# Decay differences as bf16 matmuls of cut cumulated decays, and the read decay in the same exponential

## What is computed

```python
def step(h, inp):
    x_t, dt_t, B_t, C_t = inp
    dA = jnp.exp(dt_t * A)
    h = h * dA[:, :, None, None] + jnp.einsum('bh,bhp,bn->bhpn', dt_t, x_t, B_t)
    y = jnp.einsum('bhpn,bn->bhp', h, C_t)
    return (h, y)
# both directions; NHEADS = 2, HEADDIM = 128, D_STATE = 64; dt = softplus(...)
out = (y_fw + y_bw[:, ::-1, :]) @ out_proj_w.T
```

## Time and profile before

| what | value |
|---|---|
| median of 3 runs | 424.61 us (423.61 to 426.65) |
| the profiled execution | 423.88 us |
| its span, first to last instruction | 422.2 us |
| PE busy | 381.2 us (90%) |
| DVE busy | 341.9 us (81%) |
| POOL busy | 321.2 us (76%) |
| ACT busy | 299.6 us (71%) |
| mean granted TensorE clock | 0.988 |

### The profile page before, as it was taken

One profiled execution on the slowest core, in us unless ns is written; L12 is line 12 of the kernel. 1 busy time (PEld: TensorE's weight loads), 2 busy tenths in 40 slices (PEclk: granted clock), 3 DMA queues, 4 the chain that ended last, 5 costly groups with the idle time before them and its releaser, 6 DMA issues. The chain is left out here.

```text
span 422.2 us, 10384 instructions
## 1 busy us (share of the span) xinstructions
PE 381.2 (90%) x3004; PEld 344.8 (82%) x3004; DVE 341.9 (81%) x1031; ACT 299.6 (71%) x866; POOL 321.2 (76%) x486
## 2 busy tenths in 40 slices
PE   8889989997998899699999899889998998999990
PEld 7757878897888798587889788779998887989990
DVE  6687789998879998989779998789688756768880
ACT  3776789797799988678677788898766665444430
POOL 4754894799995989679989889999947777765541
PEclk9999999999999999999999999999999999999996
DMA  8999999999940000001010110003921176888720
GB/s 228 330 334 335 334 336 331 334 334 330 325 127 2 1 2 2 0 2 50 2 53 2 50 51 3 2 0 110 379 68 39 54 216 177 264 253 234 223 78 0
DMA packets 54950, 63.27 MB, mean 150 GB/s; under 512 B 4604, under 2 KB 47996, under 8 KB 54768
## 3 DMA queue, kind: packets, MB, share of 16 engines
q1 hardware_dynamic: 50528, 55.76, 43.9%
q0 software_dynamic: 2784, 6.37, 4.1%
q10 hardware_dynamic: 1584, 0.50, 0.5%
HBM read 20.97 MB, written 42.09 MB: 149 GB/s over the span
## 5 line engine op out<-in xcount | busy, mean ns | idle before, releaser
L721 POOL TENSOR_TENSOR accb<-accb,prod 128x512 f32<-128x512 f32 x48 | 61.3, 1277 | 23.4 <-ACT accb L1144 19.4
L2036 DVE SCALAR_TENSOR_TENSOR bank<-raw,cw,bank 128x512 f32<-128x512 f32 x96 | 72.1, 751 | 2.2 <-ACT bank L1154 0.9
L754 POOL TENSOR_SCALAR lseg<-strict,av 128x128 f32<-128x128 f32 x128 | 47.8, 387 | 6.4 <-DVE av L1995 4.4
L1577 PE MATMUL bank<-skip,cx 128*128 128x128 f32 x256 | 41.2, 284 | 7.7 <-DVE st L2084 7.3
L1813 PE MATMUL bank<-raw 128*128 x312 | 43.5, 283 | 0.9 <-DVE raw L2459 0.9
L1193 ACT ACTIVATE xt<-bank,dtv 128x128 f32<-128x128 f32 x128 | 39.5, 362 | 5.2 <-PE bank L1556 4.9
L1577 PEld LDWEIGHTS bank<-skip,cx 128*128 128x128 f32 x256 | 33.6, 191 | 10.7 <-DVE st L2084 9.8
L955 POOL DMA_INDIRECT routed_rows<-rows,rowat x32 | 33.5, 1045 | 10.8 <-issue 9.1
L1051 POOL DMA_INDIRECT out_dram<-raw x26 | 25.7, 988 | 20.0 <-DVE raw L2485 13.3
L1813 PEld LDWEIGHTS bank<-raw 128*128 128x128 f32 x312 | 38.0, 192 | 1.7 <-issue 1.0
L1593 PE MATMUL bank<-xt,ms 128*128 128x128 f32 x256 | 39.0, 275 | 0.0
(11 more groups left out here) (294 smaller groups left out, 1134.8 us busy)
## 6 DMA issues: line engine op xcount, KB each, us to landing
routed_rows<-padrow SPq DMA_DIRECT2D x32, 1040.0 KB, 12.5
zs<-routed_rows SPq DMA_DIRECT2D x39, 130.0 KB, 3.3
xs<-in_w_dram SPq DMA_DIRECT2D x16, 258.0 KB, 3.6
hT<-in_w_dram SPq DMA_DIRECT2D x15, 258.0 KB
zs<-in_w_dram SPq DMA_DIRECT2D x8, 258.0 KB, 3.7
raw<-in_w_dram SPq DMA_DIRECT2D x1, 2048.0 KB, 10.0
xs<-in_u_dram SPq DMA_DIRECT2D x3, 512.0 KB, 8.2
routed_rows<-padrow SPq DMA_DIRECT2D x9, 130.0 KB, 3.2
```

What stands on the lines that cost most here:

```text
L721: pool.tensor_tensor(accb[:, :], accb[:, :], prod[:, :], ALU.add).then_inc(s_tapb, 1)
L754: last = pool.tensor_scalar(lseg[:, Q % LA, h, :], strict[:, d, :], av[:, b, col(d, h, t)], 1.0, ALU.mult, ALU.mult)
L1577: last = pe.matmul(bank[4 + Q % 2][:, h * HD:(h + 1) * HD], cx[:, S % 2, h, c0:c0 + P], skip[:, d * NH + h, :], start=(h == 0), stop=False ...
L2036: dve.scalar_tensor_tensor(out=acc(S, g)[:, :], in0=raw[:, g, c0:c0 + BLK], scalar=cw[:, d, g, k:k + 1], in1=acc(S, g)[:, :], op0=ALU.mult ...
```

## The change

The two heads' exponents are no longer made of triangles scaled on POOL. DVE rounds the decays to a grid (`round_decays`), PE cumulates the rounded and the remaining part (`cumulate`), DVE cuts the cumulated decays into four bf16 pieces (`cut_pieces`), PE transposes them in bf16 (`turn_pieces`), ACT keeps them once whole (`pc`) and once for each head with the other head's rows at zero (`pch`) (`keep_pieces`). In a chunk the exponent is then the difference of two bf16 matmuls into the same bank, 256 columns each: a 0/1 column spread over 128 by `pch` (the cumulated decay of token i), and `pc` by −1/0 (that of token j). `decay_rows`, `lseg`, `s_L`, `decay_copies`, `start_rows`, `cut_starts` and `cut_rest` go. The read decay's exponent is put beside the heads', and one exponential of 128x384 takes all three; `cs` is then a product of two SBUF tiles.

```diff
-OTHER = (1, 2, 2, 3, 5, 4, 4)
+OTHER = (1, 2, 2, 3, 5, 4, 0, 4)
# POOL
-            def decay_rows(Q):
...
-                for h in range(NH):
-                    last = pool.tensor_scalar(lseg[:, Q % LA, h, :], strict[:, d, :],
-                                              av[:, b, col(d, h, t)], 1.0, ALU.mult, ALU.mult)
-                last.then_inc(s_L, 1)
...
-                if Q + LA < NCH:
-                    decay_rows(Q + LA)
# ACT
+            def keep_pieces(b):
...
+                turned = side(u)[:, 0:P].bitcast(BF16).rearrange("p (d i) -> p d i", d=2)
+                act.activation(pc[:, b, :, :], turned, ACT.Copy)
+                for h in range(NH):
+                    last = act.activation(pch[:, b, :, h, :], turned, ACT.Copy, scale=halves[:, h:h + 1])
+                last.then_inc(free(u), 1)
...
-                act.activation(es[:, Q % 2, :, :], bank[2 + Q % 2][:, 0:DI].rearrange("p (h i) -> p h i", h=NH),
+                act.activation(es[:, Q % 2, :, :], bank[2 + Q % 2][:, 0:DI + P].rearrange("p (h i) -> p h i", h=NH + 1),
                                ACT.Exp).then_inc(s_e, 1)
...
-            start_rows_out(0)
+            keep_pieces(0)
             c_over_b(0)
# PE, once a batch
+            def cumulate(b):
...
+                pe.wait_ge(s_hilo, b + 1)
                 for d in range(2):
+                    last = pe.matmul(side(u)[:, d * 2 * W:(d + 1) * 2 * W], incl[:, d, :],
+                                     hilo[:, d].rearrange("p k c -> p (k c)"), start=True, stop=True)
+            def turn_pieces(b):
...
+                pe.wait_ge(s_cpart, b + 1)
+                for d in range(2):
+                    last = pe.transpose(side(u)[:, d * (P // 2):(d + 1) * (P // 2)].bitcast(BF16),
+                                        cpart[:, d].rearrange("p c k -> p (c k)"), identb[:, :])
# PE, prepare(Q)
-                pe.matmul(sg[:, DI:DI + P], bb[:, S % 2, c0:c0 + P], cc[:, S % 2, c0:c0 + P],
+                pe.matmul(sg[:, DI + P:DI + 2 * P], bb[:, S % 2, c0:c0 + P], cc[:, S % 2, c0:c0 + P],
                           start=True, stop=True)
-                if Q % CHUNKS == 0:
-                    pe.wait_ge(s_eparts, b + 1)
-                pe.matmul(sg[:, DI + P:DI + 2 * P], pick[:, t, :], eparts[:, b, d, :], start=True, stop=True)
+                pe.matmul(sg[:, DI:DI + P], pick[:, t, :], pc[:, b, d, :], start=True, stop=True)
                 pe.matmul(sg[:, 0:DI], identb[:, :], negm[:, d, :, :].rearrange("p h i -> p (h i)"),
                           start=True, stop=False, skip_group_check=True)
-                pe.wait_ge(s_L, Q + 1)
-                for h in range(NH):
-                    last = pe.matmul(sg[:, h * P:(h + 1) * P], lseg[:, Q % LA, h, :], incl[:, d, :],
-                                     start=False, stop=True, skip_group_check=True)
+                pe.matmul(sg[:, 0:DI], onet[:, t:t + 1].broadcast_to([P, P]),
+                          pch[:, b, d, :, :].rearrange("p h i -> p (h i)"), start=False, stop=False, skip_group_check=True)
+                last = pe.matmul(sg[:, 0:DI], pc[:, b, d, :],
+                                 minus[:, :].rearrange("p (h t) -> p h t", h=NH)[:, :, t].unsqueeze(2).broadcast_to([P, NH, P]),
+                                 start=False, stop=True, skip_group_check=True)
# DVE
+            def round_decays(b):
...
+                cut(dve.tensor_scalar(some, decay, FLOOR, None, ALU.max))
+                cut(dve.tensor_scalar(hilo[:, :, 0, :], some, GRID, GRID, ALU.add, ALU.subtract))
+                dve.tensor_tensor(hilo[:, :, 1, :], some, hilo[:, :, 0, :], ALU.subtract).then_inc(s_hilo, 1)
+            def cut_pieces(b):
...
+                dve.tensor_copy(cumd[:, :, :, :].rearrange("p d k c -> p (d k c)"), side(u)[:, 0:4 * W]).then_inc(free(u), 1)
+                wait_free(dve, u)
+                cut(dve.tensor_copy(cpart[:, :, 0, :], cumd[:, :, 0, :]))
+                cut(dve.tensor_tensor(r[1], cumd[:, :, 0, :], cpart[:, :, 0, :], ALU.subtract))
+                cut(dve.tensor_copy(cpart[:, :, 1, :], r[1]))
+                cut(dve.tensor_tensor(r[2], r[1], cpart[:, :, 1, :], ALU.subtract))
+                cut(dve.tensor_tensor(r[3], cumd[:, :, 1, :], r[2], ALU.add))
+                cut(dve.tensor_copy(cpart[:, :, 2, :], r[3]))
+                dve.tensor_tensor(cpart[:, :, 3, :], r[3], cpart[:, :, 2, :], ALU.subtract).then_inc(s_cpart, 1)
# DVE, mix(Q): cs
-                dve.tensor_tensor(cs[:, Q % 2, :], cc[:, (Q // BT) % 2, c0:c0 + P], sg[:, DI + P:DI + 2 * P],
+                dve.tensor_tensor(cs[:, Q % 2, :], cc[:, (Q // BT) % 2, c0:c0 + P], es[:, Q % 2, NH, :],
                                   ALU.mult).then_inc(s_m, 1)
# DVE, the entry
             softplus_end(0)
+            round_decays(0)
             taps_x(0, 1)
+            cut_pieces(0)
             gate_bc(0)
-            decay_copies(0)
             gate_x(0, 1)
-            cut_starts(0)
-            cut_rest(0)
             gate_z(0, 0)
```

More of the change, by code:

```diff
@@ L33 @@
 MASKED = -30000.0
+FLOOR = -110.0
+GRID = 24576.0
+NP = 4
 NTOK = B * L
@@ L556, in build @@
         NFIRST = 35
-        NCONST = 17
+        NCONST = 18
         def fresh_rows(k):
@@ L664, in _ @@
                                     pattern=[[-1, P]], channel_multiplier=1))
[L665 to L666 removed]
+            link(pool.tensor_tensor(ident4[:, :], ident[:, 0:W], ident[:, W:2 * W], ALU.add))
+            for c in range(2, NP):
+                link(pool.tensor_tensor(ident4[:, :], ident4[:, :], ident[:, c * W:(c + 1) * W], ALU.add))
             hold(pool, s_fill0, 3)
@@ L974, in cut_b2 @@
                 hold(pool, s_b2, 10)
-            for Q in range(LA):
-                decay_rows(Q)
             raw_bc_there(1)
@@ L1357, in _ @@
                 if nxt is not None and (s, j) == (7, 0):
-                    start_rows_out(nxt)
+                    keep_pieces(nxt)
                 if g is not None and j == 0:
@@ L1501, in sums @@
                 for d in range(2):
-                    for k, m in enumerate((incl[:, d, :], strict[:, d, :])):
-                        pe.matmul(side(u)[:, k * NQ + d * W:k * NQ + (d + 1) * W], m, av[:, b, d * W:(d + 1) * W],
-                                  start=True, stop=True)
+                    pe.matmul(side(u)[:, d * W:(d + 1) * W], strict[:, d, :], av[:, b, d * W:(d + 1) * W],
+                              start=True, stop=True)
                     for h in range(NH):
-                        last = pe.matmul(side(u)[h * NS:(h + 1) * NS, 2 * NQ + d * TPB:2 * NQ + (d + 1) * TPB],
+                        last = pe.matmul(side(u)[h * NS:(h + 1) * NS, NQ + d * TPB:NQ + (d + 1) * TPB],
                                          ones[:, 0:NS], av[:, b, d * W + h * TPB:d * W + (h + 1) * TPB],
@@ L1996, in softplus_end @@
                                   ALU.mult).then_inc(s_a, 1)
-            def decay_copies(b):
-                wait_free(dve, USE["pfx", b])
-                for c in range(3):
-                    last = dve.tensor_copy(e0rep[:, :, c, :], etab[:, b, 0, :].rearrange("p (d k) -> p d k", d=2))
-                last.then_inc(s_rep, 1)
-            nsp = [0]
-            def split(ins):
-                nsp[0] += 1
-                ins.then_inc(s_split, 1)
-                dve.wait_ge(s_split, nsp[0])
@@ new lines, in cut @@
+            def cut(ins):
+                ncut[0] += 1
+                ins.then_inc(s_cut, 1)
+                dve.wait_ge(s_cut, ncut[0])
+            def round_decays(b):
+                decay = av[:, b, :].rearrange("p (d c) -> p d c", d=2)
+                some = rest[:, 0, :].rearrange("p (d c) -> p d c", d=2)
+                dve.wait_ge(s_a, b + 1)
+                cut(dve.tensor_scalar(some, decay, FLOOR, None, ALU.max))
+                cut(dve.tensor_scalar(hilo[:, :, 0, :], some, GRID, GRID, ALU.add, ALU.subtract))
+                dve.tensor_tensor(hilo[:, :, 1, :], some, hilo[:, :, 0, :], ALU.subtract).then_inc(s_hilo, 1)
@@ new lines, in cut_pieces @@
+            def cut_pieces(b):
+                u = USE["cum", b]
+                r = [rest[:, k, :].rearrange("p (d c) -> p d c", d=2) for k in range(4)]
+                wait_full(dve, u)
+                dve.tensor_copy(cumd[:, :, :, :].rearrange("p d k c -> p (d k c)"), side(u)[:, 0:4 * W]).then_inc(free(u), 1)
[7 more added lines that the diff above has]
+                dve.tensor_tensor(cpart[:, :, 3, :], r[3], cpart[:, :, 2, :], ALU.subtract).then_inc(s_cpart, 1)
@@ L2333, in _ @@
                     carry(Q)
-                if nxt is not None and (s, j) == (7, 0):
-                    cut_starts(nxt)
-                if nxt is not None and (s, j) == (7, 1):
-                    cut_rest(nxt)
                 conv_b(S, j)
@@ L2381, in _ @@
                         softplus_end(nxt)
+                        round_decays(nxt)
                     if (s, j) == (6, 2):
-                        decay_copies(nxt)
```

(1 more changed line is left out.)

93 lines of the change are left out of this document (41 added, 52 removed).

## The result

The changed kernel takes 433.71 us (432.68 to 436.32), the kernel before took 424.23 us beside it on the same chip: ratio 1.0222, 95% interval 1.0159 to 1.0285. It is slower by 9.5 us where 4.4 us less were forecast. The profiled execution took 434.4 us, 432.7 of them its span, 10.5 more than before.

What follows compares the result with a forecast made beforehand. PE was taken as first bound of the chunks, DVE second, ACT in the chain between; −10.6 + 1.7 − 1.6 + 0.3 + 3.8 + 2.0 = −4.4 us gave 420.2 us against 424.61, range 412 to 430.

Steps and rivals of the forecast that it cites:

- PE, −10.6: Chunks: two bf16 matmuls replace two fp32, 14.1 us less stream, three quarters counted: −10.6 us; bounds −4.7 and −14.1.
- The second batch: Its preparation: eleven small DVE instructions for ten, three on ACT for one, 0.8 us; a quarter, 0.2 us, left out.
- The clock: Entry only: TensorE's lower clock level may last longer; upper bound +4.0 us if it reaches the first chunks.
- Hold, +3.8: Chunks: cs, now from two SBUF tiles, held by POOL's sums, 11 times, 7.6 us; half counted, +3.8 us.
- the wider rule: Skill's rule that POOL scalings hold cs too: 10.8 us of holds instead of 7.6, forecast 1.6 us later.
- Entry, +2.0: Entry: new DVE and ACT work before gate_bc and c_over_b delays the first exponential: +2.0 us, bounds +1.0 and +4.0.
- ACT, +1.7: Chunks: exponential grows from 256 to 384 columns, 6.8 us, a quarter counted: +1.7 us; bounds 0 and 6.8.
- POOL, −1.6: Chunks: 128 scalings go, so sums come earlier; half of ACT's 3.3 us wait: −1.6 us; bounds 0 and some −5.
- Rival C: Hold of cs in mix decides; 20 hits on the path cost 13.8 us: slower, 430.2 us; chance 0.17.
- Its point of decision: Rival C: kernel slower than before once more than 8.2 us of holds on cs are on the path.

Runs made afterwards that it cites:

- e7: Changed kernel with the cumulated decays in the bank of the prefix sums, copied out by ACT: ratio 1.0136 to the kernel before.
- e16: Changed kernel plus keep-warm matmuls in four places where PE waited and its clock fell: ratio 1.0304 to the kernel before.
- e17: The hybrid plus keep-warm matmuls at chunks 16, 26, 43 and before the turning of the second batch's pieces: ratio 1.0196 to the kernel before.
- the fill: Two extra bf16 matmuls of 256 columns per chunk, results overwritten, giving PE the stream of before; costs 1.1 to 1.2% in the changed kernel.
- e2: Changed kernel plus two extra bf16 matmuls of 256 columns per chunk: ratio 1.0327 to the kernel before.
- the hybrid: Changed kernel with entry and second batch reordered, read decay as exponentials in three bf16 pieces, cs reading PSUM, all values kept: ratio 1.0010 to the kernel before.
- e13: The hybrid plus two extra bf16 matmuls of 256 columns per chunk: ratio 1.0144 to the kernel before.
- e8: Changed kernel with cs reading the read decay's exponent from PSUM, plus two extra bf16 matmuls per chunk: ratio 1.0314 to the kernel before.
- e1: Changed kernel with cs reading its second input, the read decay's exponent without exponential, from PSUM, so no hold: ratio 1.0085 to the kernel before.
- e15: Changed kernel with one bank for both sums and only the second batch's preparation moved: ratio 1.0120 to the kernel before.
- e14: Changed kernel with only the entry reordered, gate_bc(0) before cut_pieces(0), c_over_b(0) before keep_pieces(0): ratio 1.0138 to the kernel before.
- e10: Changed kernel with entry and second batch reordered and cs reading the read decay's exponent from PSUM: ratio 1.0059 to the kernel before.
- e9: Changed kernel, arithmetic and hold kept, with entry and second batch reordered and one bank for both sums: ratio 1.0063 to the kernel before.

## Why the prediction was wrong

I forecast −4.4 us and measured +9.5. The sizes of single instructions were right; what failed is how much of each reaches the end, and what had been left out. To divide the result I fitted the time from first to last ms of the 19 traces above by six things (e7's bank as half of the second batch's order): 0.45 us for each us of low clock (±0.08), hold 1.8 (±0.9), old order of the second batch 2.8 (±0.8), PE's shorter stream −4.2 (±0.8), 128 more columns 0.9 (±1.0), POOL's scalings gone +1.9 (±1.0). For the changed kernel, 0.45 × 13.7 + 1.8 + 2.8 − 4.2 + 0.9 + 1.9 = 9.4, where its trace, one of the 19, shows 285.5 − 276.4 = 9.1. A fit is weaker than a single experiment: it misses a trace by 1.4 us on average, the last two sizes can hardly be told from nothing, and it takes the clock for a cause of its own. Without e16 and e17, whose extra matmuls cost something themselves, the sizes move by 0.7 at most.

- **PE, −10.6: the step that failed.** The stream is 14.1 us shorter as worked out, but "three quarters count" was wrong: the fill is worth 5 us in the change (e2) and in the hybrid (e13), the lower bound I gave. Only e8 over e1 gives three quarters, with the low clock in it. I had argued from idle totals (20 against 36 us); the earlier trace rows already had PE waiting 7.3 us for DVE's state, and this wait grew by 8.9 us: it took the rest.
- **The second batch, "left out", 0.2 us: the other step that failed.** Moving it is worth 4 us (e15). I counted eleven instructions against ten, and did not follow the new bank through PE's queue: whom "cum" waits for, and that y_turn waits behind it for DVE's copy.
- **The clock.** I allowed for it at the entry alone. Four low stretches in the chunks cost some 6 us by the fit, and stand at waits of PE. Two of these waits are longer than in the kernel before (2.58 and 2.14 us against 1.64 and 1.60), the one for cumd is new, and the fourth is shorter (2.13 against 2.43), so what brings a stretch about stays open. They overlap with the other items: hold and order also count through them.
- **Hold, +3.8.** 17 held cs and 7.05 us against 11 and 7.6. Its price is 1.8 by the fit, 5 us when removed alone, perhaps none in the new order. My term lies in between, and its mechanism is shown, though wider than I had it: only 9 of the 17 stand under sums L728. The reading of the earlier trace rows, that scalings don't hold, was wrong, and so was the size of the wider rule: in the kernel before, 14 cs start inside an L716 or L907 with 5.4 us of them left, so it would have been 13.0 us, not 10.8.
- **Entry, +2.0.** First exponential +2.3 us. That its order is worth 3 us (e14) I had not seen, though "gate_bc behind cut_pieces" was in my own sum; only 1 us of them is at the entry.
- **ACT, +1.7**: 0.9, within its bounds. **POOL, −1.6**: nothing, or up to +1.9 by the fit; the relieved POOL only waits longer for ACT's first tap, the bound of 0 that I named.

Rival C (430.2) is nearest in time and sign. Its point of decision, 8.2 us of holds on the path, was not reached: there were 7.05 in all, and the kernel was slower already, since PE's gain was half as large as C assumed and two costs were missing. So that C's number is near is in part luck. The range ended at 430, 3.7 us short.

## What to carry to other kernels

If an engine waits for another's result in every turn of a loop, shortening its stream fills those waits first: count a third, not three quarters, until a filler has measured it (here 5 of 14.1 us). A once-per-batch preparation of a microsecond costs several if it takes a shared buffer in turn with the main loop; follow the new buffer's releases through each queue. Try an addition's order before judging it: here the order alone was 1.4% of a 2.2% loss.

## What the runs showed of the hardware that I had not expected

- A DVE product of two SBUF tiles can also be held under POOL instructions with a single SBUF input: 0.48 us under L723, 0.36 us under L694, in place of 0.28; under POOL sums it takes up to 1.37 us (269.22). Where it isn't held, the POOL scaling is the longer: L907 1.60 in place of 0.79 us in the kernel before.
- TensorE's granted clock falls within a loop in which PE is busy 88% of the time; it did so at waits of 2.12 to 2.58 us, and four matmuls then take 1.06 in place of 0.61 us. The length of the wait doesn't settle it: the kernel before had one of 2.43 us (103.4) and no low stretch, and e1, e10 and e17 had waits of 2.45 to 2.52 us with none.
- The hold and the low clock did not add up: removing the hold alone gave 5 us, removing it after the order was mended gave 0.2 us of time (e10 against e9).
